# Four mask products ahead of four score products in the masked attention of a one-core Flamingo block

## The chip, the cores and the metric

The kernel runs on one core of a Trainium2 chip. The metric is the device time of one execution in microseconds. The engines of the core work side by side and meet through semaphores: TensorE (PE in the profile, its weight loads PEld), VectorE (DVE), ScalarE (ACT), GpSimd (POOL) and the queue of SyncE (SP), which here only starts transfers.

## What is computed

Four batches of 512 tokens with 256 features pass through four blocks in a row: a cross attention with 16 heads of 64, a grouped attention with a mixture of experts, a masked cross attention with 16 heads of 16 against 1601 context rows, and a self attention with experts. The change is in the third block:

```python
def _L1_xattn_ref(values, keys, queries, mask, w_out, b_out):
    ...
    energy = jnp.einsum('nqhd,nkhd->nhqk', q, k)
    energy = jnp.where(mask == 0, jnp.float32(-1e+20), energy)
    attn = jax.nn.softmax(energy / math.sqrt(EMBED), axis=3)
    out = jnp.einsum('nhql,nlhd->nqhd', attn, v).reshape(N, q_len, HEADS * HEAD_DIM)
    return out @ w_out.T + b_out
```

## The kernel before

The program is one list of units (`plan.order`), written once by `build_order`, and every engine walks through it in that order, each doing its own part of a unit. So the list is the order of the work on TensorE, and an engine that waits holds up everything behind it on that engine. `build_order` has generators, each a stream of units (scores of a block, products with the values, what prepares them), and `weave` takes from them by a string of digits: `TURNS_1` for the blocks 1 and 2, `TURNS_3` for the blocks 3 and 4, one digit for each unit. `Pace` keeps estimated times beside it (`Step(...)`: TensorE time, time on other engines, slots). They decide which of the three slots a unit takes (the one that comes free first) and how many `warm` products fill long gaps, not the order itself.

The scores and projections of all blocks share three slots of PSUM, the ring (`RING = 3`), each of two banks of 512 columns. A slot is free again when ScalarE or VectorE has read it.

Of block 3, for each of four batches and four groups of four heads:

- `max3` (32 units for a group): two heads' products of 128 queries with 401 keys in bf16, L1227, one slot; VectorE adds the mask and takes the maximum (L1679, two instructions for a unit), which frees the slot.
- `negb`, `strip`, `low`, `rowb` (L1219, L1246): make the row with the negated maxima, which goes into the queries as an extra feature.
- `scoreb` with blk 3, the masked tile (13 for a group, 208 in all): scores of up to 124 keys with 512 queries for four heads, in two slots, two heads in each. The heads' score products (L1266, 32 rows of the array for each head, fp32, two instructions for a product) run side by side in the four row strips. The mask is added by a product with a unit matrix on the whole array in bf16: L1259 for the heads 0 and 1, ahead of the scores, and L1272 for the heads 2 and 3, behind them. The wait for the second slot (`second_free`) stands between the score products of head 1 and head 2. ScalarE then takes the exponentials, one instruction for a slot (L1435).
- `pvb` with blk 3 (13 for a group): the product with the values, four heads in four strips of 32 columns (L1287). It takes no slot. It runs a tile or two behind the scores, since there are two buffers for exponentials.

Block 4 is woven into it, a batch behind: `maxb` (L1239), its own `scoreb` without a mask (4 for a group, the same L1266 with keys in `wide`), its `pvb`, and long stretches of whole-array products: `projqk` (L1195, L1196), `expert4` (L1366, L1367), `outb` (L1301).

TensorE works in three ways here: on the whole array, in four row strips (L1227, L1239, L1266) and in four column strips (L1287). Between two units of different ways it stands at a border, which the planner reckons with `DIVIDE`.

The tile in the code of before:

```python
                        for h in range(2):
                            pe.matmul(head_bank(unit, h), ident_b[0:kn, :], maskT_sb[0:kn, k, :],
                                      start=True, stop=False)
```

Of the kernel before, what the change touches and what calls it, by code (L numbers as in the profile page):

```python
# [21 lines left out]
GROUP = 4  # L22
PAD = P // GROUP
PAIRS = HEADS // 2
# [100 lines left out]
class Slots:  # L125
# [33 lines left out]

TURNS_3 = (
    "00333333333333333333333333333333333333333133301323132331332313231323313323133231332313233133233213031332332133"
    "13323133233133231332313323133233231333133233231102313323313323213310332331332313332313323133231332331332332130"
    "31332121032132332133133231323313323133231323313323133231332313023332133331023133233213323013412332114343323734"
    "27313341323413323132336142337132334231434334132334214734371323313323545324471363532441336413323134241435323313"
    "36532323336413343413423132313233321371363532353633133231332314231323313323133253634323431314243143532313323132"
    "33321336437146353241323313324142337471323536413231323332136341343343532353233361125363321363325713635323313633"
    "43612313233321124331343323733413424734132341332371423413324132341332361342334371335323313243713635332337136343"
    "34241335323414243713235323414365323363411323413234133256536341423413324133253641323413423333643331743243532341"
    "13233136353323413323361323371323332153234136337132341332532333413341423523361133653231323633713235323136313231"  # L170
    "32332513633436123142132334323173341334421424132413241323413324132314233725417142436132314235323413364133654241"
    "32413635323371323132333321433313231323332654171324146353235324471363313233713243713231324132337132413235363233"
    "43613314254125716546241421654214212446124121425216521125616225764644746447447447474744554645464546444674455464"
    "5464546444674454546445446464546575656576676"
)

# [140 lines left out]
def build_order(plan):  # L318
# [52 lines left out]
    def wide_prep():  # L371
        for b in range(B):
            for p in range(PAIRS):
                s, before = p % 2, pair_at(b, p, -2)
                gate = (("pva", *before, NKT - 1),) if before else ()
                if p == 0:
                    yield Step(use=(("ve", 4.2),), needs=gate, name=("ln", 1, b))
                    emit(on(("ln", 1, b), *free["xn_a"]))
                    yield Step(1.0, (("sc", 1.05),), 1, (("ln", 1, b),), ("turn", 1, b))
                    turn = emit(on(in_slot(("turn", 1, b), "scalar"), *free["xnT_a"]))  # L380
                    free["xn_a"] = (("tensor", turn),)
                for c in range(2):
                    yield Step(2.75, (("sc", 0.9), ("ve", 0.6)), 1, gate, ("kproj", b, p, c))
                    emit(on(in_slot(("kproj", b, p, c), "scalar"), *k_free[s], *free["kB"]))
                yield Step(1.75, (("sc", 0.6), ("ve", 0.45)), 1, (("turn", 1, b),), ("qproj", b, p))
                unit = emit(on(in_slot(("qproj", b, p), "scalar"), *k_free[s], *free["qB"]))
                if p == PAIRS - 1:
                    free["xnT_a"] = (("tensor", unit),)
                for q in range(QT):
                    for c in range(4):  # L390
                        yield Step(0.17, (("ve", 1.05),), 1, (("qproj", b, p),), ("maxa", b, p, q, c), (2, 2))
                        unit = emit(in_slot(("maxa", b, p, q, c), "vector"))
                free["kB"] = free["qB"] = (("tensor", unit),)
                yield Step(use=(("ve", 0.3),), needs=(unit,), name=("nega", b, p))
                emit(on(("nega", b, p), *free["col_a"]))
                yield Step(0.25, (("sc", 0.6),), 1, (("nega", b, p),), ("rowa", b, p))
                unit = emit(on(in_slot(("rowa", b, p), "scalar"), *neg_free[s]))
                free["col_a"] = (("tensor", unit),)
# [101 lines left out]
    def slim_scores(blk, b, g):  # L500
        tiles = NKT if blk == 3 else QT
        expo, before = {2: expo_2, 3: expo_3, 4: expo_4}[blk], group_at(b, g, -1)
        masks = (2.0, (1, 1), 1.5, 0.55) if blk == 3 else (0.88, (4, 4), 0.88, 0.0)
        for k in range(tiles):
            unit = ("scoreb", blk, b, g, k)
            behind = (b, g, k - 2) if k >= 2 else (*before, tiles + k - 2) if before else None
            yield Step(masks[0], (("sc", 1.02), ("sc", 1.02)), 2,
                       (("rowb", blk, b, g),) + ((("pvb", blk, *behind),) if behind else ()), unit, *masks[1:])
            in_slots(unit, "scalar_first", "scalar")
            i = expo.take()  # L510
            plan.slot[unit], plan.slot_free[unit] = i, expo.free[i]
            emit(unit)
        if blk != 2:
            (k3_free if blk == 3 else k4_free)[g % 2] = (("tensor", unit),)
# [241 lines left out]
def flamingo(nc, t, out):  # L756
    plan = Plan()
    order, bank_of, slot_of = plan.order, plan.bank, plan.slot
    ctx = ExitStack()
    with ctx:  # L760
# [216 lines left out]
        def head_bank(unit, h):  # L977
            return ring_t[:, bank_of[unit][h // 2], (h % 2) * BANK:(h % 2 + 1) * BANK]
# [94 lines left out]
        def _(pe):  # L1073
            past = Past(pe)
            past.wait_ge(*at("vector", "setup"))
            for unit in order:
# [171 lines left out]
                elif kind == "scoreb":  # L1248
# [6 lines left out]
                        past.wait_ge(*(at("scalar", "projk", b) if blk == 2 else at("scalar", "projqk", b, g)))  # L1255
                    if blk == 3:
                        past.wait_ge(*at("vector", "mask_keys"))
                        for h in range(2):
                            pe.matmul(head_bank(unit, h), ident_b[0:kn, :], maskT_sb[0:kn, k, :],  # L1259
                                      start=True, stop=False)  # L1260
                    for h in range(GROUP):
                        own = slice(PAD * h, PAD * h + PAD)
                        if h == 2:
                            for lane, other in plan.second_free[unit]:
                                past.wait_ge(*at(lane, *other))
                        last = pe.matmul(head_bank(unit, h), key_columns(blk, g, k0)[own, :],  # L1266
                                         queries_place(blk, g)[own, :], start=blk != 3 or h >= 2, stop=blk != 3 or h < 2)
                        if h == 1:
                            last.then_inc(tensor_done, 1)
                    if blk == 3:  # L1270
                        for h in range(2, GROUP):
                            last = pe.matmul(head_bank(unit, h), ident_b[0:kn, :], maskT_sb[0:kn, k, :],  # L1272
                                             start=False, stop=True)
                    last.then_inc(tensor_done, 1)
                elif kind == "pvb":
                    blk, b, g, k = a
# [679 lines left out]
```

## Time and profile before

| | us |
|---|---|
| median of 3 runs | 3478.32 (3477.23 to 3482.04) |
| the profiled execution | 3479.19 |
| its span | 3477.0 |
| first masked tile starts, last ends, from the span's start | 2127.6, some 3331 |
| PE busy | 3308.9 (95%) |
| DVE busy | 2020.1 (58%) |
| ACT busy | 1439.3 (41%) |

All rows come from the one profiled execution. A group's "busy" counts overlapping instructions of the group once, and a matmul's end is modelled, so the distance from start to start tells more of TensorE's pace than its busy share.

### The profile page before, as it was taken

To read this page: it belongs to the slowest core of one execution; us is meant where nothing else is said; L and a number is where in the kernel's file an instruction comes from.
4 is the path that set the end of the run, shared out by engine and by line. 5 is a ranking of instruction groups with operands and counts; after the bars stand their busy time and mean duration, and the time that the engine had idled before them with its cause. 6 is when DMAs were issued, how large, how long until landed. Compare 5 with 4: busy or idle time off the path is not lost.

```text
span 3477.0 us, 45530 instructions
## 1 busy us (share of the span) xinstructions
PE 3308.9 (95%) x18530; PEld 1442.0 (41%) x18530; DVE 2020.1 (58%) x4314; ACT 1439.3 (41%) x1645; POOL 957.2 (28%) x469
## 2 busy tenths in 40 slices
PE   7999999999999999999997979998999999999999
PEld 4444444444444445434442752223323343333354
DVE  4444445554665465565565027776767677666546
ACT  3443434444334443344433212454454435544434
POOL 4665555454465553554500000110000000000000
PEclk9999999999999999999999999999999999999999
DMA  4000000000000000000021430211111111110000
GB/s 154 11 13 13 32 8 11 13 7 32 8 19 11 13 26 8 25 10 8 4 97 49 125 108 18 60 39 49 35 35 36 35 29 25 51 35 26 13 19 13
DMA packets 68252, 114.94 MB, mean 33 GB/s; under 512 B 4849, under 2 KB 49545, under 8 KB 67530
## 3 DMA queue, kind: packets, MB, share of 16 engines
q1 hardware_dynamic: 62666, 97.08, 8.8%
q0 software_dynamic: 5376, 14.95, 1.9%
q8 instruction: 145, 2.38, 0.3%
q14 instruction: 65, 0.53, 0.0%
HBM read 101.79 MB, written 16.78 MB: 34 GB/s over the span
## 4 chain that ended last, share of the span: by engine, by line
PE 85%; DVE 7%; ACT 4%; POOL 2%; DMA 1%; issue 1%; ACTq 0%; DVEq 0%; POOLq 0%
PE ring L1266 10%; PE pv L1160 10%; PE ring L1149 9%; PE pv L1287 9%; PE ring L1227 3%; PE ring L1259 3%; PE ring L1121 3%; PE ring L1130 3%; PE ring L1122 3%; PE ring L1146 3%; PE ring L1107 3%; PE ring L1272 2%; PE ring L1108 2%; ACT wide L1435 2%; PE ring L1345 2%; PE ring L1326 2%
## 5 line engine op out<-in xcount | busy, mean ns | idle before, releaser
L1532 POOL TENSOR_TENSOR wide<-wide 124x1024 f32<-124x1024 f32 (+1 forms) x341 | 804.2, 2358 | 263.9 <-ACT wide L1428 227.7
L1435 ACT ACTIVATE wide<-ring 124x1024 f32<-124x1024 f32 (+2 forms) x544 | 528.5, 1022 | 549.4 <-PE ring L1266 547.0
L1651 DVE TENSOR_REDUCE max_a<-ring 128x2 f32<-128x802 f32 x512 | 491.9, 991 | 373.0 <-PE ring L1130 372.8
L1428 ACT ACTIVATE wide<-ring 124x1024 f32<-124x1024 f32 (+1 forms) x416 | 425.6, 1027 | 445.5 <-PE ring L1149 404.3
L1679 DVE CUSTOM_DVE_ANT_0 rest<-ring,slim 128x401 bf16<-128x401 f32 x683 | 374.3, 577 | 138.1 <-PE ring L1227 134.2
L1149 PE MATMUL ring<-wide 64*124 64x512 f32 (+1 forms) x1664 | 428.6, 593 | 0.0
L1160 PE MATMUL pv<-wide 124*64 124x512 f32 (+1 forms) x1664 | 413.0, 611 | 3.5 <-ACT wide L1428 3.5
L1689 DVE TENSOR_REDUCE slim<-ring 128x2 f32<-128x1024 f32 x256 | 307.5, 1221 | 111.6 <-PE ring L1239 110.3
L1266 PE MATMUL ring<-slim 32*128 32x512 f32 x2176 | 351.1, 646 | 3.0 <-DVE max_b L1679 2.3
L1502 POOL DMA_DIRECT2D slim<-in_ctx_k x16 | 8.8, 549 | 992.8 <-PE ring L1227 628.6
L1529 POOL TENSOR_TENSOR wide<-wide 124x1024 f32<-124x1024 f32 x31 | 73.4, 2369 | 557.9 <-ACT wide L1428 435.7
L1287 PE MATMUL pv<-wide,slim 124*32 124x512 f32 (+1 forms) x1664 | 223.8, 611 | 0.9 <-ACT wide L1435 0.9
L1679 DVE CUSTOM_DVE_ANT_0 slim<-ring,slim 128x401 bf16<-128x401 f32 x341 | 196.1, 575 | 46.9 <-PE ring L1227 45.4
L1160 PEld LDWEIGHTS pv<-wide 124*64 124x64 f32 (+1 forms) x1664 | 98.7, 136 | 225.4 <-issue 206.0
L1149 PEld LDWEIGHTS ring<-wide 64*124 64x124 f32 (+1 forms) x1664 | 156.7, 185 | 73.2 <-issue 50.2
L1227 PE MATMUL ring<-slim 32*128 32x401 bf16 x1024 | 157.8, 340 | 14.4 <-ACT wide L1435 10.7
L1130 PE MATMUL ring<-wide 64*128 64x401 bf16 x1024 | 154.8, 338 | 16.0 <-DVE max_a L1651 10.2
L1146 PE MATMUL ring<-wide,select_b 64*128 64x512 bf16 x832 | 160.1, 382 | 10.3 <-DVE max_a L1651 5.7
L1266 PEld LDWEIGHTS ring<-slim 32*128 32x128 f32 x2176 | 110.8, 184 | 139.5 <-issue 110.9
L1121 PE MATMUL ring<-wide 128*124 128x128 f32 (+1 forms) x832 | 165.9, 282 | 2.5 <-ACT wide L1424 1.8
L1122 PE MATMUL ring<-wide 128*124 128x128 f32 (+1 forms) x832 | 162.6, 277 | 0.0
L1435 ACT ACTIVATE slim<-ring 128x1024 f32<-128x1024 f32 x128 | 124.4, 1021 | 87.3 <-PE ring L1266 86.7
(239 smaller groups left out, 4096.2 us busy)
## 6 DMA issues: line engine op xcount, KB each, us to landing
slim<-in_ctx_k SPq DMA_DIRECT2D x16, 800.5 KB, 4.3
wide<-in_w_pair SPq DMA_DIRECT2D x32, 384.0 KB, 3.1
slim<-in_ctx_v SPq DMA_DIRECT2D x16, 744.0 KB
wide<-in_w SPq DMA_DIRECT2D x16, 512.0 KB, 4.8
wide<-in_we SPq DMA_DIRECT2D x16, 512.0 KB, 3.7
wide<-in_ctxT SPq DMA_DIRECT2D x4, 1601.0 KB, 6.6
slim<-in_ctx_k POOLq DMA_DIRECT2D x16, 400.2 KB, 4.7
wide<-padded_x SPq DMA_DIRECT2D x8, 640.0 KB, 4.8
```

What stands on the lines that cost most here:

```text
L1121: pe.matmul(place, ctxT[:, 0, k0:k0 + kn], pair_weights(p)[:, 2, 0, :], start=True, stop=False)
L1122: last = pe.matmul(place, ctxT[:, 1, k0:k0 + kn], pair_weights(p)[:, 2, 1, :], start=False, stop=True)
L1149: last = pe.matmul(slot[0:kn, h * BANK:(h + 1) * BANK], keys_a[own, p % 2, k0:k0 + kn], queries_a[own, p % 2, :], start=False, stop=True)
L1160: last = pe.matmul(pv_a[64 * h:64 * h + 64, :], values_a[0:kn, p % 2, k, 64 * h:64 * h + 64], exps_a[0:kn, slot_of["scorea", b, p, k], h * ...
L1266: last = pe.matmul(head_bank(unit, h), key_columns(blk, g, k0)[own, :], queries_place(blk, g)[own, :], start=blk != 3 or h >= 2, stop=blk ...
L1287: last = pe.matmul(pv_of[blk][PAD * h:PAD * h + PAD, :], value_columns(blk, g, k, kn, h), exps_tile(blk, b, g, k, h)[0:kn, :], start=k == ...
L1428: sc.activation(exps_a[0:kn, slot_of[unit], :], slot[0:kn, :], ACT.Exp, scale=WIDE ** -0.5).then_inc(scalar_done, 1)
L1435: sc.activation((exps_2 if blk == 2 else exps_34)[0:kn, first + 2 * i:first + 2 * i + 2, :].rearrange("p h n -> p (h n)"), ring_t[0:kn, ba ...
L1532: po.tensor_tensor(sums[0:kn, :], sums[0:kn, :], view, ALU.add).then_inc(pool_done, 1)
L1651: ve.reduce_max(max_a[:, :, q, c], slot.rearrange("p (h n) -> p h n", h=2)[:, :, 0:CHUNK], AX.X).then_inc(vector_done, 1)
L1679: ve.tensor_tensor_reduce(out=max_junk[junk], in0=slot[:, i * BANK:i * BANK + CHUNK], in1=maskQ_sb[:, q, CTX_CHUNKS[c]:CTX_CHUNKS[c] + CHUNK],
L1689: ve.tensor_reduce(neg_cols[blk][:, q, 2 * hp * PAD:2 * hp * PAD + PAD + 1:PAD], slot.rearrange("p (h n) -> p h n", h=2), AX.X, ALU.max, n ...
```

## The change

Of a masked tile all four mask products come first, then all four score products. The wait for the second slot moves with it, ahead of the mask product of head 2. The planner's entry for the tile is 1.86 instead of 2.0, its way of working at the end is four strips instead of the whole array, its first scores are counted from 1.86 instead of 1.5, and its second slot from 0.42 instead of 0.55. `TURNS_3` is another string. In `wide_prep` the first keys of a batch get one more condition (`held`) for the planner.

```diff
-        masks = (2.0, (1, 1), 1.5, 0.55) if blk == 3 else (0.88, (4, 4), 0.88, 0.0)
+        masks = (1.86, (1, 4), 1.86, 0.42) if blk == 3 else (0.88, (4, 4), 0.88, 0.0)
...
+                held = (("vproj", b - 1, PAIRS - 1, 1),) if b and p == 0 else ()
...
-                    yield Step(2.75, (("sc", 0.9), ("ve", 0.6)), 1, gate, ("kproj", b, p, c))
+                    yield Step(2.75, (("sc", 0.9), ("ve", 0.6)), 1, gate + held, ("kproj", b, p, c))
...
 TURNS_3 = (
-    "00333333333333333333333333333333333333333133301323132331332313231323313323133231332313233133233213031332332133"
...
+    "00333333333333333333333333333333333333333133313233132331332332313331323313323313323132331323032312330331332313"
...
                     if blk == 3:
                         past.wait_ge(*at("vector", "mask_keys"))
-                        for h in range(2):
+                        for h in range(GROUP):
+                            if h == 2:
+                                for lane, other in plan.second_free[unit]:
+                                    past.wait_ge(*at(lane, *other))
                             pe.matmul(head_bank(unit, h), ident_b[0:kn, :], maskT_sb[0:kn, k, :],
                                       start=True, stop=False)
                     for h in range(GROUP):
                         own = slice(PAD * h, PAD * h + PAD)
-                        if h == 2:
+                        if h == 2 and blk != 3:
                             for lane, other in plan.second_free[unit]:
                                 past.wait_ge(*at(lane, *other))
                         last = pe.matmul(head_bank(unit, h), key_columns(blk, g, k0)[own, :],
-                                         queries_place(blk, g)[own, :], start=blk != 3 or h >= 2, stop=blk != 3 or h < 2)
+                                         queries_place(blk, g)[own, :], start=blk != 3, stop=True)
                         if h == 1:
                             last.then_inc(tensor_done, 1)
-                    if blk == 3:
-                        for h in range(2, GROUP):
-                            last = pe.matmul(head_bank(unit, h), ident_b[0:kn, :], maskT_sb[0:kn, k, :],
-                                             start=False, stop=True)
                     last.then_inc(tensor_done, 1)
```

In the blocks 1 and 2 the order and the slots are as before. In the blocks 3 and 4 the number of each kind of unit is the same, except for two more `warm` units (together one product more).

Two places show the order on TensorE. The line numbers of the changed kernel: L1263 is the mask products, L1270 the score products, L1228 the maxima, L1287 the values still; an x2 of L1228 is one `max3` unit, an x4 two.

TensorE, batch 0, group 3, from the masked tile 3 on, before:

```order
L1259 MATMUL ring<-slim,ident_b 128x512 x2
L1266 MATMUL ring<-slim 128x512 x4
L1272 MATMUL ring<-slim,ident_b 128x512 x2
L1227 MATMUL ring<-slim 128x401 x2
L1287 MATMUL pv<-wide,slim 32x512 x4
L1227 MATMUL ring<-slim 128x401 x4
L1259 MATMUL ring<-slim,ident_b 128x512 x2
L1266 MATMUL ring<-slim 128x512 x4
L1272 MATMUL ring<-slim,ident_b 128x512 x2
L1227 MATMUL ring<-slim 128x401 x4
L1287 MATMUL pv<-wide,slim 32x512 x4
L1227 MATMUL ring<-slim 128x401 x2
```

The same tiles with the change:

```order
L1263 MATMUL ring<-slim,ident_b 128x512 x4
L1270 MATMUL ring<-slim 128x512 x4
L1228 MATMUL ring<-slim 128x401 x2
L1287 MATMUL pv<-wide,slim 32x512 x4
L1228 MATMUL ring<-slim 128x401 x4
L1263 MATMUL ring<-slim,ident_b 128x512 x4
L1270 MATMUL ring<-slim 128x512 x4
L1228 MATMUL ring<-slim 128x401 x2
L1287 MATMUL pv<-wide,slim 32x512 x4
L1228 MATMUL ring<-slim 128x401 x2
```

The scores now stand directly against the maxima, with no mask product between, and of the maxima one instead of two comes right behind a tile; two and three maxima for a tile take turns, where before most tiles of this place had three.

TensorE, batch 1, group 1, where a tile of block 4's scores (the L1270 with `wide`) follows a masked tile, with the change (before, this place had the same units between such a pair, at a tile two later in the group):

```order
L1263 MATMUL ring<-slim,ident_b 128x512 x4
L1270 MATMUL ring<-slim 128x512 x4
L1228 MATMUL ring<-slim 128x401 x2
L1287 MATMUL pv<-wide,slim 32x512 x4
L1228 MATMUL ring<-slim 128x401 x2
L1270 MATMUL ring<-wide 128x512 x4
```

Here the unit that follows takes two slots at once and starts both with its first products; it moved two tiles forward.

## Rows read from the trace of the kernel before

**Rows 1.** The page's busy line of TensorE: us, share, instructions.

```profile
PE 3308.9 (95%) x18530; PEld 1442.0 (41%) x18530; DVE 2020.1 (58%) x4314; ACT 1439.3 (41%) x1645; POOL 957.2 (28%) x469
```

**Rows 2.** Busy time of each engine in the masked half, granted clock, DMA share, GB/s.

```profile
2125.00:3332.00 1207.00, 1170.94 (x7045) 409.88 (x7043) 827.75 (x2532) 569.70 (x616) 31.75 (x38) 0.99 0.13 35
```

**Rows 3.** Groups by line in that stretch: busy us, mean ns, idle before, releasers.

```profile
L1435 ACT ACTIVATE wide<-ring 124x1024 f32<-124x1024 f32 (+2 forms) x510 | 495.5, 1022 | 535.6 <-PE ring L1266 533.4 <-PE ring L1272 1.7
...
L1266 PE MATMUL ring<-slim 32*128 32x512 f32 x1664 | 267.9, 643 | 2.3 <-DVE max_b L1679 2.3
...
L1227 PE MATMUL ring<-slim 32*128 32x401 bf16 x960 | 146.8, 340 | 13.9 <-ACT wide L1435 10.7 <-DVE slim L1710 1.2 <-DVE max_b L1679 0.5
L1272 PE MATMUL ring<-slim,ident_b 124*128 124x512 bf16 (+1 forms) x416 | 126.8, 387 | 0.0
L1259 PE MATMUL ring<-slim,ident_b 124*128 124x512 bf16 (+1 forms) x416 | 125.9, 384 | 4.5 <-ACT wide L1435 2.8 <-DVE max_b L1679 1.2
```

**Rows 4.** TensorE in order of time: start us, us, line, instructions, idle before and releaser.

```profile
2322.45 0.60 PE L1259 MATMUL ring<-slim,ident_b 124*128 124x512 bf16 x2
2322.99 1.14 PE L1266 MATMUL ring<-slim 32*128 32x512 f32 x8
2324.06 0.61 PE L1272 MATMUL ring<-slim,ident_b 124*128 124x512 bf16 x2
2324.60 0.34 PE L1227 MATMUL ring<-slim 32*128 32x401 bf16 x2
2324.87 1.07 PE L1287 MATMUL pv<-wide,slim 124*32 124x512 f32 x8
2325.87 0.69 PE L1227 MATMUL ring<-slim 32*128 32x401 bf16 x4
2326.49 0.60 PE L1259 MATMUL ring<-slim,ident_b 124*128 124x512 bf16 x2
2327.03 1.50 PE L1266 MATMUL ring<-slim 32*128 32x512 f32 x8
2328.45 0.60 PE L1272 MATMUL ring<-slim,ident_b 124*128 124x512 bf16 x2
...
2330.88 0.60 PE L1259 MATMUL ring<-slim,ident_b 124*128 124x512 bf16 x2
...
2333.73 0.34 PE L1227 MATMUL ring<-slim 32*128 32x401 bf16 x2 [0.29 <-ACT wide L1435]
```

**Rows 5.** ScalarE in the same stretch: both exponentials of the first two tiles.

```profile
2324.22 1.94 ACT L1435 ACTIVATE wide<-ring 124x1024 f32<-124x1024 f32 x2 [2.45 <-PE ring L1266]
2328.26 1.94 ACT L1435 ACTIVATE wide<-ring 124x1024 f32<-124x1024 f32 x2 [2.10 <-PE ring L1266]
```

**Rows 6.** VectorE there: first and last instruction of one unit of maxima.

```profile
2324.98 0.58 DVE L1679 CUSTOM_DVE_ANT_0 rest<-ring,slim 128x401 bf16<-128x401 f32 x1 [1.17 <-PE ring L1227]
...
2325.98 0.08 DVE L1679 DVE_READ_ACCUMULATOR2_ANT max_b<- 128x1 f32 x1
```

**Rows 7.** TensorE later: a mask pair with a whole-array product behind it.

```profile
2519.85 0.60 PE L1272 MATMUL ring<-slim,ident_b 124*128 124x512 bf16 x2
2520.29 1.02 PE L1219 MATMUL ring<-slim,consts 128*128 128x512 f32 x2
```

**Rows 8.** TensorE: unmasked scores of block 4 with maxima right behind them.

```profile
2509.61 1.14 PE L1266 MATMUL ring<-wide 32*128 32x512 f32 x8
2510.58 0.34 PE L1227 MATMUL ring<-slim 32*128 32x401 bf16 x2
```

**Rows 9.** TensorE: a masked tile and the block-4 tile that follows it.

```profile
2646.19 0.60 PE L1259 MATMUL ring<-slim,ident_b 124*128 124x512 bf16 x2
...
2649.84 1.22 PE L1266 MATMUL ring<-wide 32*128 32x512 f32 x8
```

**Rows 10.** TensorE's waits in the masked half: waiter, releaser, us, times, longest.

```profile
PE ring L1227 <- ACT wide L1435: 10.7, 32, 1.0
```

More of the change, by code:

```diff
@@ L161 @@
 TURNS_3 = (
-    "00333333333333333333333333333333333333333133301323132331332313231323313323133231332313233133233213031332332133"
[L163 to L171, printed above, removed]
@@ L172 @@
-    "32413635323371323132333321433313231323332654171324146353235324471363313233713243713231324132337132413235363233"
-    "43613314254125716546241421654214212446124121425216521125616225764644746447447447474744554645464546444674455464"
-    "5464546444674454546445446464546575656576676"
+    "00333333333333333333333333333333333333333133313233132331332332313331323313323313323132331032312330331332332313"
+    "33321331323313323313323323112013233133323023333110332331332313233133323321333133233133233133233133231332331230"
@@ new lines @@
+    "12312313233132331323313233321331332313233132313233103231323313321230331323313233132331332332133132330412334121"
+    "32331333432337461423413241423431424333413231323313234323413331323533313233143241323353365423734136341323433714"
+    "64334532333641323313235334132341363532341323353327136331323413353241323334142343744314243413231323132313633657"
+    "52323371364132313241463325713231323132413231323536413233637134333532331363532353233713631323132353631323363713"
+    "32336341421213234323373341334132373413241323313234132436142341324132343234134532313637132313233132437132335343"
@@ new lines @@
+    "43341323532437136413241324313635323132336571323332513633132331323373734132353464331231424314243413241323136353"
+    "23132431323365713231363323413353243713241324132313241324132413245132314633335324313233132313633265713635323532"
+    "31363136353231323633436412121323433374363347341324142341324132471423313343254132331363532414233132353231463413"
+    "23413233713233136433752433341324334132331323365217132313241324132413233132353631323136353235324136413241323334"
+    "14234412657121752121421426456121421421421462452146571625756257664644746447444744747445546454645464446744554645"
@@ L175 @@
+    "4645464446744745445446546454646575656576676"
 )
```

## The prediction

> **What bounds the kernel now.** The page's first section comes first: TensorE is busy for 95% of the span [rows 1], so the end is set there, and what counts is its pace and its waits. The change reorders only the half with blocks 3 and 4, so the next view is the table of stretches for the masked half: 1207 us, TensorE busy for 1170.94, VectorE 827.75, ScalarE 569.70 [rows 2]. That looks like an engine with nothing to give but its own work, but the groups by line say otherwise. The score products are busy for 267.9 us over 208 tiles, 1.29 us for a tile [rows 3], where an undisturbed tile shows 1.14 [rows 4]: 0.15 us for a tile, some 31 us, are a wait inside the tile, for the second slot, and the view of waits counts none of it, as busy time is modelled. The waits that it does count are small, the longest sum 10.7 us in 32 times [rows 10]. So two things share the limit: TensorE's own sequence, and the three slots of the ring.
>
> The timeline of TensorE shows both. From start to start a tile is 0.54 for the first mask pair, 1.07 for the scores, 0.54 for the second pair, 2.15 in all [rows 4]. Where whole-array work follows the second pair, the pair costs 0.44 [rows 7], and where maxima follow scores directly, the scores cost 0.97 [rows 8]. A border between two ways of working is thus some 0.10 us. One maxima unit is 0.27, one unit of the value products 1.00 [rows 4]. The next tile in that series waits: its scores take 1.50 busy instead of 1.14 [rows 4], for lack of the second slot.
>
> **What the change takes away on TensorE.** No product is added or removed. Two of the three borders around a tile may go. After the change a tile is 0.54 for the first masks, 0.44 for the other two (the price of a pair with its own kind behind), then 0.97 with maxima or unmasked scores behind, 1.07 with anything else: 1.95 or 2.05. Before, it is 2.15, or 2.05 with whole-array work behind. Which unit follows I counted in the two orders. Before: in 153 of 208 tiles strip work (maxima nearly always), in 18 value products, in 37 whole-array products: 171 x 2.15 + 37 x 2.05 = 443.5 us. After: 182 strip work, 18 value products, 8 whole-array: 182 x 1.95 + 26 x 2.05 = 408.2 us. The difference is 35.3 us. Whole-array units that stood behind a tile for free now stand elsewhere and bring borders of their own: the orders hold 1394 borders in this half before and 1064 after, 330 fewer, where the tiles alone lose 353. The 23 others give 2.3 us back. So 33.0 us of TensorE's sequence are gone, if nothing waits.
>
> **What it does to the ring.** A slot is held until it is read. Before, from the tile's start, the first exponential begins at 1.77 (2324.22 against 2322.45) and the two end at 3.71 [rows 4, 5]. A maxima unit that waited for the first slot began 2.85 after its tile (2333.73 against 2330.88) [rows 4], so slot one is free at 2.85, and slot two at 3.71 and the same 0.06 of passing on, 3.77. After the change the scores start 0.44 later, and both exponentials with them: 3.29 and 4.21. Slot two is also wanted sooner, at 0.44 instead of 0.54, since its masks come early. A tile holds its slots for 0.44 + 0.44 + 0.10 = 0.98 us longer, 204 us for 208 tiles, which over three slots is 68 us of the ring, twice what TensorE saves. What of it comes onto the path depends on what stands between two tiles, and I walked through the patterns. A maxima unit holds its slot from its start to the end of VectorE's last instruction, 1.46 (2326.06 against 2324.60) [rows 4, 6], 1.51 with passing on.
>
> Two maxima between tiles (scores, maxima, values, maxima; 43 times after, 19 before). Before: 2.15 + 0.27 + 1.00 + 0.27 = 3.69, and slot two is free at 3.77: a cycle of 3.77. After: 1.95 + 1.54 = 3.49, first slot at hand, second wanted at 3.93 and free at 4.21: 0.28 of waiting, again 3.77. The saving is gone whole.
>
> Two and three in turn, the first place shown in the change (three: 42 with the third behind the values, 5 otherwise). Before: after 3.77 the second cycle reaches 7.73, wants its second slot at 8.27 and has it at 8.70 when the second maxima unit is read: 8.16 for two. After: the second cycle would start at 7.60, waits for slot two until 7.98, then for the slot of the second maxima unit (free at 8.57, wanted at 8.42): 8.13. For three each time the trace has 4.39 (2330.88 against 2326.49) [rows 4], and the same walk gives 4.36 after. So 90 tiles of such short cycles lose 90 x 0.20 = 18.0 us of the saving and keep 90 x 0.015 = 1.3.
>
> A block-4 tile behind a masked one, with maxima, values, maxima between (17 after, 13 before). It takes two slots at once. Before it starts 3.65 after its masked tile and can have slot two at 3.77 [rows 9]; after, it stands ready at 3.49 and its heads 2 and 3 wait until 4.21. That loses the 0.20 and another 0.44: 17 x 0.64 = 10.9 us. This term is the least sure: its bounds are 17 x 0.20 = 3.4 us (other waits would have come anyway) and twice the 10.9, where the late block-4 tile makes the next masked one late too.
>
> The other tiles, some 100, stand in cycles with long whole-array stretches (experts, projections) or with the values alone; slots are free long before they are wanted there, and the saving stays.
>
> **Edits without a price.** The first half has the same order and the same slots, so the extra condition there costs nothing. ScalarE and VectorE do the same work; their busy sums in the masked half (569.70 and 827.75 of 1207 us) [rows 2] leave cover for any shift in their order. One warming product more is 0.2 us. Of the gathers and the low keys on GpSimd's queue one swap is made, with transfers that have many us to land at a DMA share of 0.13 [rows 2]. The buffers of keys and values are released by tiles whose order in their own stream is the same. The granted clock is 0.99 in this stretch [rows 2], the upper of the two levels (2.4 GHz), and nothing here lets TensorE rest longer.
>
> **The sum.** 33.0 - 18.0 + 1.3 - 10.9 = 5.4 us gained. Against the profiled execution, 3479.2, that is 3473.8, and since its time is 0.9 over the median of the runs, 3473 against 3478.3.
>
> **A rule that speaks against the change.** What the rows show is that the time from a score product to a free slot is ScalarE's, 1.94 us for two slots [rows 5], whatever TensorE does. The Trainium skill says it under TensorEngine Tiling, section PSUM Bottleneck, in my words: packing products into strips speeds the array, but not the reading of PSUM, which may become the limit. By that rule alone the masked half would not gain at all, which is the second rival; by the borders alone it would gain the whole 33 us, the first.
>
> **Rivals.** First: the ring does not take it back, because the new order was made with the tile's longer hold in mind and my walk takes every short cycle at its tightest. For it: two maxima between tiles stand where three stood, and one instead of two right behind the tile, so that fewer maxima wait for the first slot (the 10.7 us in 32 times [rows 10]). Against it: the walk of the very order shown ends at 8.13 and 8.16. It gives 25 to 33 us, about 3450.
>
> Second: reading sets the pace, the gain is wholly gone. The short cycles as above, and in the long ones the time freed before a stretch is waited off behind it. It gives no change, 3478.
>
> Third, slower: the wait for slot two, now ahead of all scores, delays both exponentials where before it delayed only the second. A late slot then makes the next slot late, and so on through a row of short cycles. The place is the masked tile's third mask product, above all behind block-4 tiles. Its price is the mean wait inside a tile: today 0.15 us. The saving of 33 us is 0.16 for a tile, so from a mean wait of 0.31 us on the change costs. My walk has 0.28 in the cycle with two maxima and 0.38 + 0.15 in the one with three, so it is near. At 0.40 for all tiles it is 208 x 0.25 - 33 = 19 us slower, 3497; at 0.35, 3487. Against it: half of the tiles are not in short cycles.
>
> That the change does not do what it says would be a border that stays between masks and scores of the same tile; that one is counted. The other borders vanish by construction.
>
> **How the numbers follow.** My forecast, most of the saving waited off, 3464 to 3481 around 3473: 0.45. First rival, 3445 to 3464: 0.17. Second, 3475 to 3482: 0.16. Third, 3485 to 3500: 0.22. A difference of 0.2%, 7 us, is about what a measurement of this kernel can tell from none. Of the forecast's case somewhat over half lies more than 7 us below, with the first rival 0.42 faster; slower is the third rival and a little of the forecast, 0.24; the rest is 0.34. For the range I take in the first rival down to 3447 and the third up to 3493, which leaves a tenth on either side.
>
> **What would show it.** In the profile after: a score group of 0.97 from start to start with maxima behind it, and mask groups of four with 0.98 to the scores; both exponentials 2.2 after the tile's start instead of 1.77; in the first place a pair of cycles of 8.1 us. Waits of TensorE for the exponentials move from the maxima into the mask products: over 30 us of idle time or stretched groups there. The masked half as a whole ends 5 us sooner. Wrong would be: tiles whose masks take no longer than 0.98 nearly everywhere (then the gain is near 33), or a mean stretch of the mask group by more than 0.3 (then it is slower).

## The result, and the profile after

The changed kernel takes 3524.44 us in the median (3518.02 to 3527.61) against 3477.78 for the kernel before: a ratio of 1.0134, 95% interval 1.0121 to 1.0146. It is 46.7 us slower, where 5 us faster was forecast and the range ended at 3493.

The masked half in the profile after, the table of stretches (us; busy time of each engine; clock; DMA), answers to [rows 2]; it lasts from 2128.1, the first masked tile, to some 3367:

```profile
2125.00:3369.00 1244.00, 1153.13 (x7002) 396.61 (x7001) 834.80 (x2530) 562.52 (x611) 32.03 (x39) 0.98 0.13 34
```

TensorE is busy for 1153 us instead of 1171, in a stretch that is 37 us longer. The granted clock is 0.98 against 0.99; what stands behind that small difference comes at the end of this section. The groups by line of that stretch (busy us, mean ns, idle before and releasers), to hold against [rows 3]:

```profile
L1270 PE MATMUL ring<-slim 32*128 32x512 f32 x1664 | 244.9, 659 | 0.0
L1263 PE MATMUL ring<-slim,ident_b 124*128 124x512 bf16 (+1 forms) x832 | 243.2, 391 | 40.0 <-ACT wide L1435 30.2 <-DVE max_b L1679 7.4
...
L1228 PE MATMUL ring<-slim 32*128 32x401 bf16 x960 | 149.4, 338 | 38.9 <-ACT wide L1435 34.1 <-DVE max_b L1679 3.0 <-ACT src L1400 0.6
```

Masks and scores together are busy for 488.1 us, where they were for 520.6. The idle time before masks rose from 4.5 to 40.0 us and before maxima from 13.9 to 38.9, and most of it (64.3 of the 78.9 us) ends with an exponential of ScalarE. Part of the rise before the masks is only the tile's old wait made visible: before, the wait for the second slot stood inside the scores, where idle time does not show it. The waits of TensorE by releaser (total us, times, longest), against [rows 10]:

```profile
PE ring L1228 <- ACT wide L1435: 34.1, 39, 1.7
PE ring L1263 <- ACT wide L1435: 30.2, 52, 4.2
```

The view of waits still leaves out what hides inside a group. So I took every unit's start in the trace and set against each distance the shortest one that the same kind of neighbours shows; what is over counts as a wait. The split between the two depends by a few us on which distances are compared. From the first masked tile's start to the last one's, the kernel before has 1200.1 us, of which 147.3 are waits; the changed one has 1235.6, of which 219.6 are waits. TensorE's own sequence went from 1052.8 to 1016.0 us, 36.8 less, and the waits rose by 72.3. Behind the last masked tile's start the span has 149.4 us before and 159.8 after, another 10.4.

The series that the forecast walked through, batch 0, group 3, shows TensorE (start us, us, line, instructions, idle):

```profile
2350.06 1.25 PE L1263 MATMUL ring<-slim,ident_b 124*128 124x512 bf16 x4
2351.24 1.14 PE L1270 MATMUL ring<-slim 32*128 32x512 f32 x8
2352.21 0.33 PE L1228 MATMUL ring<-slim 32*128 32x401 bf16 x2
2352.48 1.06 PE L1287 MATMUL pv<-wide,slim 124*32 124x512 f32 x8
2353.55 0.52 PE L1228 MATMUL ring<-slim 32*128 32x401 bf16 x4
2354.46 1.21 PE L1263 MATMUL ring<-slim,ident_b 124*128 124x512 bf16 x4 [0.40 <-ACT wide L1435]
...
2358.20 1.03 PE L1263 MATMUL ring<-slim,ident_b 124*128 124x512 bf16 x3
```

and ScalarE beside it:

```profile
2352.47 1.94 ACT L1435 ACTIVATE wide<-ring 124x1024 f32<-124x1024 f32 x2 [1.83 <-PE ring L1270]
2356.84 1.94 ACT L1435 ACTIVATE wide<-ring 124x1024 f32<-124x1024 f32 x2 [2.44 <-PE ring L1270]
```

The scores cost 0.97 with maxima behind them. The two cycles take 4.40 and 3.74, 8.14 together (8.13 was forecast). The masks of both tiles are stretched by a late second slot (1.18 and 1.15 to the scores instead of 0.97), and the first exponential comes 2.41 and 2.38 after the tile's start, against 1.77 in [rows 5]; a tile that gets its slot in time shows 2.20. So here the walk was right. The loss is elsewhere, for instance where two maxima follow a tile:

```profile
2148.68 1.14 PE L1270 MATMUL ring<-slim 32*128 32x512 f32 x8
2149.64 0.33 PE L1228 MATMUL ring<-slim 32*128 32x401 bf16 x2
2150.99 0.50 PE L1228 MATMUL ring<-slim 32*128 32x401 bf16 x4 [1.01 <-ACT wide L1435]
2151.91 1.21 PE L1263 MATMUL ring<-slim,ident_b 124*128 124x512 bf16 x4 [0.41 <-ACT wide L1435]
```

The second maxima unit can only have the tile's first slot, and stands for 1.01 us; in [rows 4] the same place stood for 0.29 (2333.73). Then the next tile stands for another 0.41.

Not everything that I counted as a wait is one. The records of the granted clock have 27.3 us at 0.50 in the masked half before and 54.6 us after. One such stretch of the changed kernel, with TensorE in it:

```profile
2227.40:2237.60 10.20, 8.54 (x34) 1.88 (x38) 6.55 (x27) 1.94 (x2) 0.00 (x0) 0.50 0.00 1
```

```profile
2228.21 0.52 PE L1228 MATMUL ring<-slim 32*128 32x401 bf16 x2 [2.34 <-DVE max_b L1679]
2228.66 1.89 PE L1263 MATMUL ring<-slim,ident_b 124*128 124x512 bf16 x4
2230.48 2.09 PE L1270 MATMUL ring<-slim 32*128 32x512 f32 x8
```

Just before, TensorE had stood for 1.68 and 2.34 us. The tile then takes 3.69 us from start to start (to 2232.35) instead of 1.95, on the lower of the two levels (1.2 instead of 2.4 GHz). Of the waits above, some 26 us of the 219.6 lie in stretches at 0.50, and 10 of the 147.3 before, so up to 16 of the 72 us more are products at the lower level that came with the new waits.

### The profile page after: what moved, and what is told of

It is laid out like the page before. It is cut to its first block, busy times and chain, and to the rows that moved or that the text cites. A ratio compares the mean times of both kernels' runs of the same rounds, so it can differ in the third digit from the quotient of the medians.

```text
span 3523.5 us, 45530 instructions
## 1 busy us (share of the span) xinstructions
PE 3300.5 (94%) x18531; PEld 1432.9 (41%) x18531; DVE 2027.9 (58%) x4314; ACT 1435.1 (41%) x1643; POOL 956.7 (27%) x469
## 3 DMA queue, kind: packets, MB, share of 16 engines
q8 instruction: 145, 2.38, 0.3%
## 4 chain that ended last, share of the span: by engine, by line
PE 82%; DVE 8%; ACT 6%; issue 1%; POOL 1%; DMA 1%; SPq 0%; DVEq 0%; ACTq 0%; POOLq 0%
PE ring L1270 11%; PE pv L1161 10%; PE ring L1150 9%; PE pv L1287 7%; PE ring L1263 6%; ACT wide L1435 4%; PE ring L1122 3%; PE ring L1131 3%; PE ring L1123 3%; PE ring L1147 3%; PE ring L1108 3%; PE ring L1109 2%; PE ring L1228 2%; PE ring L1345 2%; PE ring L1326 2%; PE ring L1366 2%
## 5 line engine op out<-in xcount | busy, mean ns | idle before, releaser
L1270 PE MATMUL ring<-slim 32*128 32x512 f32 x2176 | 328.0, 658 | 0.7 <-DVE slim L1704 0.4
L1263 PE MATMUL ring<-slim,ident_b 124*128 124x512 bf16 (+1 forms) x832 | 243.2, 391 | 40.0 <-ACT wide L1435 30.2
L1287 PE MATMUL pv<-wide,slim 124*32 124x512 f32 (+1 forms) x1664 | 224.9, 613 | 0.0
L1228 PE MATMUL ring<-slim 32*128 32x401 bf16 x1024 | 160.7, 338 | 39.4 <-ACT wide L1435 34.1
L1228 PEld LDWEIGHTS ring<-slim 32*128 32x128 bf16 x1024 | 47.5, 92 | 279.6 <-ACT wide L1435 173.7
```

Source lines behind the costliest of these rows:

```text
L1228: last = pe.matmul(slot[:, i * BANK:i * BANK + CHUNK], queries_low(3, g)[own, q * P:(q + 1) * P], keys_low(3, g)[own, CTX_CHUNKS[c]:CTX_CH ...
L1287: last = pe.matmul(pv_of[blk][PAD * h:PAD * h + PAD, :], value_columns(blk, g, k, kn, h), exps_tile(blk, b, g, k, h)[0:kn, :], start=k == ...
```

## Experiments: the form and the order apart

Three theories stood against each other. A, the ring: exponentials that start 0.44 us later bring waits that cost more than the borders give. B, the order: the tile's new form is good, the new order is bad. C, the moved wait: since the masks of heads 2 and 3 now stand ahead of all scores, a late second slot holds up the first exponential too, which the planner does not know (`Pace.accept` adds the wait to the tile's end, but counts the first exponential from the tile's start).

**The form alone.** The tile as in the changed kernel, string of turns and planner numbers as before, so that order and slots are those of before (the diff is against the changed kernel, cut):

```diff
-    "00333333333333333333333333333333333333333133313233132331332332313331323313323313323132331323032312330331332313"
+    "00333333333333333333333333333333333333333133301323132331332313231323313323133231332313233133233213031332332133"
...
-        masks = (1.86, (1, 4), 1.86, 0.42) if blk == 3 else (0.88, (4, 4), 0.88, 0.0)
+        masks = (2.0, (1, 1), 1.5, 0.55) if blk == 3 else (0.88, (4, 4), 0.88, 0.0)
```

> All four mask products ahead of the scores, but with the order and the slots of the kernel before (its string of turns and its planner numbers). Theory A (the ring: exponentials start 0.44 us later, so slots come free later, and the waits that this brings are more than the 33 to 37 us that TensorE saves): no faster than before, between 3480 and 3525 us, with the sum of borders gone and more waiting of maxima for the first exponential. Theory B (the new order is to blame, the form is good): faster than before by most of the borders, 3445 to 3460.

Measured: 3583.14 us, ratio 1.0293 (1.0271 to 1.0315), 105 us slower than before. Theory B in its plain form is refuted, and A's own figure was too small by more than half. Its waits from 2120 to 3345 us (its masked half ends at some 3436):

```profile
PE ring L1228 <- ACT wide L1435: 73.7, 87, 1.7
PE ring L1263 <- ACT wide L1435: 18.7, 42, 1.1
```

**The order alone.** The new string of turns with the tile of before (the diff is the mirror image of the last, without the tile's code).

> The new order with the tile as before (two masks, four scores, two masks). Theory A: the order is made for a tile whose slots come late and suits the old tile no worse than its own old order, 3475 to 3495. Theory B: the order itself has the loss, so the old tile in it is as slow as or slower than the changed kernel, 3520 to 3560, since the borders come back on top.

Measured: 3507.10 us, ratio 1.0076 (1.0058 to 1.0093), 29 us slower. That lies between the theories. Of these 29, the part behind the last masked tile's start is 161.1 against 149.4 us, so 12, and the masked half is 17.5 longer (1217.6 against 1200.1), of which 12 to 17 are waits, by the distances compared. The new order is thus a poor one for the old tile, but the form costs 105 in the old order and only 17 in the new.

| | old order | new order |
|---|---|---|
| two masks, scores, two masks | 3478 | 3507 |
| four masks, scores | 3583 | 3524 |

**Late exponentials alone.** The kernel before, with nothing changed on TensorE; the first exponential waits for the tile's end:

```diff
-                        past.wait_ge(*at(("tensor_first", "tensor")[i], *unit))
+                        past.wait_ge(*at(("tensor" if blk == 3 else "tensor_first", "tensor")[i], *unit))
```

> The kernel before in everything that TensorE does, but the first exponential of a masked tile waits until the whole tile is done, not for its heads 0 and 1, so both exponentials come 0.4 to 0.5 us later, as in the changed kernel. Theory A: this delay alone costs 25 to 60 us, 3503 to 3538. Theory B: ScalarE is idle half of the time, the delay is covered, under 7 us.

Measured: 3582.55 us, ratio 1.0296 (1.0279 to 1.0313), 104 us slower, where theory A's span ended at 60. Both exponentials begin 0.54 us later here (2.24 to 2.31 after the tile's start in an undisturbed tile, against 1.70 to 1.77), and a tile then costs 0.50 us more on average. ScalarE is idle for more than half of the masked half, and that covers next to nothing of it. The waits by releaser (2120 to 3345 us again) show the same place as with the form alone:

```profile
PE ring L1227 <- ACT wide L1435: 66.5, 87, 1.5
PE ring L1259 <- ACT wide L1435: 10.0, 30, 0.6
```

This run is the proof for the main point: nothing but the start of the exponentials was changed, and the kernel loses 104 us. The form alone, with the same order and the same slots, ends within 1 us of it, although it has fewer borders. The busy time of TensorE, 1194.52 us with late exponentials and 1165.75 with the masks first in the same stretch of 1310 us, does not measure that, since it holds the waits inside the scores. By starts, TensorE's own sequence is 33 us shorter with the masks first and its waits are 31 us longer. But the two are no clean pair for the borders: the delay is 0.43 us with the form alone and 0.54 here, the form alone also has the moved wait (next run), and it wants the second slot 0.10 sooner. Nor do the parts add up. An estimate in proportion to the delay gives 104 x 0.43 / 0.54 = 83 us, with 20 for the moved wait and 33 off for the borders 70, where the form alone costs 105. What makes the other 35 stays open.

**The wait alone.** The kernel before, with the second slot's wait ahead of head 0's score product:

```diff
-                        if h == 2:
+                        if h == (0 if blk == 3 else 2):
```

> The kernel before with one wait moved: the wait for the second slot of a masked tile stands ahead of the score product of head 0, no longer between heads 1 and 2. TensorE issues the same products in the same order, and a tile that gets its slot in time is unchanged; in the 100 tiles that wait there (32 us in all) the first exponential is now late by the wait as well. Theory C (the planner lets the first exponential run on during the wait, while with the masks first it cannot): 15 to 40 us slower, 3493 to 3518. Theory A in its plain form (only the fixed 0.44 us counts): within 7 us of before.

Measured: 3501.07 us, ratio 1.0056 (1.0040 to 1.0073), 20 to 23 us slower, within theory C's span. The products, their order and the price of an undisturbed tile are those of before. So theory C holds as a part of the loss, measured with the old tile in the old order: to let 100 late tiles hold up their first exponential too costs about two thirds of what those waits themselves are. The groups by line show the wait, which was invisible inside the scores (267.9 busy, 2.3 idle [rows 3]), as idle time, and maxima that wait longer:

```profile
L1266 PE MATMUL ring<-slim 32*128 32x512 f32 x1664 | 238.6, 643 | 24.2 <-DVE max_b L1679 19.0 <-ACT wide L1435 2.9 <-DVE slim L1689 0.8
...
L1227 PE MATMUL ring<-slim 32*128 32x401 bf16 x960 | 151.2, 341 | 26.5 <-ACT wide L1435 23.4 <-DVE slim L1710 1.5 <-DVE max_b L1679 0.5
```

## Experiments: the delay taken away

**Short exponentials.** Kernel before and changed kernel, both with exponentials of block 3 that take 384 of 1024 columns of a slot, so that most of the result is left out:

```diff
-                                      ring_t[0:kn, bank_of[unit][i], :], ACT.Exp,
+                                      ring_t[0:kn, bank_of[unit][i], 0:wide_c], ACT.Exp,
```

> The kernel before, but the exponentials of block 3 take only 384 of the 1024 columns of a slot, so part of the result is left out and ScalarE frees each slot some 0.6 us sooner. Only the base for the next one; with TensorE's sequence as the limit in most places, 3450 to 3475.

> The changed kernel with the same short exponentials (part of the result left out). Theory A and C: with slots that come free in time the saving of the borders shows, so it is 20 to 37 us faster than the kernel before with short exponentials, where with full ones it is 46 us slower. Theory B (the new order is bad in itself): still slower than that one, by 10 us or more.

Measured: 3461.36 us for the kernel before so shortened, ratio to the true one 0.9949 (0.9933 to 0.9966), and 3475.54 for the changed kernel, 0.9990 (0.9981 to 1.0000). The changed kernel is then 14 us slower instead of 47: two thirds of its loss hang on the time that ScalarE holds a slot. The expected gain of 20 to 37 did not come; 14 us slower is what theory B had said (10 or more), so ScalarE's hold of the slots is not the whole cause. Between the starts of the first and the last masked tile it is 1182.4 us against 1184.6, a gain of 2, and the rest behind it is 163.4 against 149.6, a loss of 14. In that rest stand 7.5 us of work that the new order puts there (below), and 28.7 us at a granted clock of 0.50 against 13.4.

The view of waits names the masks that wait for maxima, which VectorE has to read:

```profile
PE ring L1263 <- DVE max_b L1680: 26.8, 60, 1.5
```

In the kernel before with short exponentials the like of it (its L1259) is 3.9 us. But that is again the hidden wait made visible: there the scores are busy for 280.2 us in place of some 237 (208 tiles of 1.14). By starts, the waits inside the masked tile are nearly alike, some 47 us before and 52 after. What grew is the waiting of maxima behind maxima, from some 16 to 46 us. So even with a fast ScalarE this form in this order does not gain. How much of the 14 us is the order and how much the form no run separates, as the new order was not run with the old tile and short exponentials.

**Masks last.** The same borders can go in the other way: four scores first, four masks behind them, the first exponential after the masks of heads 0 and 1.

```diff
...
+                                         queries_place(blk, g)[own, :], start=True, stop=blk != 3)
...
+                    if blk == 3:
+                        for h in range(GROUP):
+                            last = pe.matmul(head_bank(unit, h), ident_b[0:kn, :], maskT_sb[0:kn, k, :],
+                                             start=False, stop=True)
+                            if h == 1:
+                                last.then_inc(tensor_done, 1)
```

> The order and slots of before; the four score products come first and all four mask products behind them, heads 0 and 1 signalled after their masks. The same borders are saved as in the changed kernel (about 33 us), the first exponential should begin about 1.8 us after the tile's start, as before (1.77), the second slot is wanted 0.54 us sooner. Theory A: most of the saving stays, 3445 to 3470. Theory B says nothing against it either, but by it e1 is as fast.

Measured: 3556.01 us, ratio 1.0222 (1.0205 to 1.0239), 78 us slower; the expectation missed. A tile with its slots in time does show its first exponential at 1.72, but the median is 2.19: the second slot is wanted at once, and 162 of 208 tiles wait for it inside the scores, 105 us in all against 35 in the kernel before. The groups by line show it as busy time of the scores (its L1263), 336.3 us against 267.9 [rows 3]:

```profile
L1263 PE MATMUL ring<-slim 32*128 32x512 f32 x1664 | 336.3, 642 | 8.1 <-ACT wide L1434 3.5 <-DVE max_b L1678 3.1
```

**Other orders.** I mended the planner so that a late second slot delays the first exponential, searched an order in which each tile may have either form, and another with all masks first.

```diff
-                end += max(0.0, self.ring[self.picked[1]] - at - step.second)
+                stall = max(0.0, self.ring[self.picked[1]] - at - step.second)
+                end += stall
+                if step.parts == (1, 4):
+                    at += stall
```

> The planner is mended so that a late second slot delays the first exponential of a tile with its masks first, and under it a new order is searched in which each of the 208 tiles may have either form; 56 take the masks first. What is asked is whether the form can be used with profit somewhere. If a saved border is worth its 0.1 us where slots are not wanted at once, 3465 to 3480, within 10 us of the kernel before; if the form costs wherever it stands, 3490 or more.

> All 208 tiles with the masks first, as in the changed kernel, and its order searched on under the mended planner. Theory C (the planner's blind spot led the order astray): it gets back part of the 46 us, 3495 to 3518, and no order of this kind reaches the kernel before, since the slots are held longer in any of them. If the order was at fault alone, below 3478.

Measured: 3499.37 us for the mixed one, ratio 1.0059 (1.0043 to 1.0076), and 3538.24 for masks first throughout, 1.0168 (1.0151 to 1.0185). The second is slower than the changed kernel itself, so the blind spot of theory C is real, but it is not shown that it led the order astray: a planner that knows of it picked a worse order. Nor does the mixed one show that the form costs wherever it stands, as was expected from 3490 up: its order is new as well, and was not run with the old tile. In its profiled execution (3491.85 us) the masked half is 7 us longer than before, and the rest behind it 8. No order that I tried makes the form pay, and none beats the kernel before. Whether one exists is open.

## Why the prediction was wrong, point by point

**TensorE's borders.** 33.0 us were forecast. The sequence in the masked half is 36.8 shorter by the trace, some 7 of it moved behind the last masked tile (below). With the old order and the form alone, where nothing moved, it is 33 shorter. This term held.

**The delay.** 0.44 us for both exponentials: 2.20 against 1.77 in an undisturbed tile. Held, in size; what it costs was not.

**The short cycles.** 8.13 forecast, 8.14 measured in the place shown. Over all cycles of two maxima, from the last score product of one tile to that of the next, 3.72 us before and 3.75 after; of three with one in front, 4.43 and 4.54. From start to start the two average 3.69 and 4.55 after the change, 8.24 for a pair, 0.1 over the forecast, so that the one place agrees to 0.01 us is in part luck. Held within some 0.1.

**The block-4 tile behind a masked one.** Its heads 2 and 3 were to come 0.44 us later, counted from the start of the masked tile. Over the places with maxima, values, maxima between, the last score product of the block-4 tile comes 4.33 us after that start before (13 places) and 4.88 after (17), 0.55 more. The place was right, the size a little small. All waits inside block-4 tiles rose from 5.3 to 17.8 us.

**The step that failed** is "The other tiles, some 100, stand in cycles with long whole-array stretches (experts, projections) or with the values alone; slots are free long before they are wanted there, and the saving stays." It was never read from rows. Some 20 of them are not even such tiles, but have two maxima right behind the tile. And the slots are not free in time. The cleanest measure is the form alone against the kernel before, as both have the same units between the same tiles. How much longer a cycle from tile to tile has become depends on the instruction it is counted from, so here are two:

| what stands between | cycles | longer, start to start | longer, last score product to last |
|---|---|---|---|
| whole-array work | 67 | 0.56 us each, 37.7 in all | 0.59 each, 39.5 in all |
| two maxima at once, short | 48 | 0.79, 38.0 | 0.84, 40.2 |
| maxima, values, maxima | 19 | 0.08, 1.6 | 0.18, 3.5 |
| other short ones with maxima | 39 | 0.43, 16.7 | 0.12, 4.7 |
| a block-4 tile | 22 | 0.39, 8.5 | 0.45, 9.9 |
| values alone, or nothing | 12 | 0.10, 1.1 | 0.49, 5.9 |

Where a saving of 0.20 each was forecast, the cycles with whole-array work lose 0.56 each (0.63 with late exponentials alone). The pattern that the walk had come out even, maxima, values, maxima, does so nearly. I had priced the patterns that stand most often in the new order, and let the rest have no price, although the prediction had itself worked out that a tile holds its slots 0.98 us longer, 68 us of the ring in all and twice what TensorE saves. That the new waits are 72 us is chance: the form alone holds the slots for just as much longer, and its waits rise by some 137. In the trace of the changed kernel they are: maxima behind maxima 39.3 to 58.9, inside the masked tile 34.6 to 51.2, masks behind maxima 4.6 to 21.3, block-4 tiles 5.3 to 17.8, and small ones.

**The clock.** The words "nothing here lets TensorE rest longer" failed with it: the new waits are such rests, and the time at 0.50 in the masked half doubled, 27.3 to 54.6 us (88.7 with the form alone; 64.8 with late exponentials alone, where TensorE's products are those of before).

**The work behind the last masked tile.** "Edits without a price" left out what the new order puts there: TensorE's lines from the end of the last masked tile hold 80 instead of 72 products of L1366 and 152 instead of 136 score products of block 4. That is one expert's unit and two tiles of block 4 with their values, 7.5 us by their rows, and the stretch is 10.4 longer; it also has 19.5 us at a granted clock of 0.50 against 13.7. I compared the counts of units for the whole half, where they are equal, and not for its end.

**The rivals.** The third had the mechanism: the wait ahead of all scores delays both exponentials. Its point from which the change costs, a mean wait of 0.31 us inside a tile, was meant for that wait alone. The trace has 51.2 us in the masks of 208 tiles, 0.25. That is below that point, and below the 0.3 that the prediction had named as the sign of a slower kernel. Yet it costs, since of the 72 us of new waits only 17 are inside the tile; the others are outside it, for its slots, by maxima and by block 4. By rights it should have been priced by everything that waits for the tile's slots. The first rival, that the order takes up the longer hold, is half true: it takes up 59 of the 105 us that the form costs in the old order. The second, no change at all, had the reading of slots as what sets the pace, but that reading also came later, which makes it a loss. Part of the 46.7 us is not the form's: the order alone costs 29 with the old tile, 12 of them behind the last masked tile.

**The rule on reading PSUM** (the Trainium skill, TensorEngine Tiling (Array Packing), section PSUM Bottleneck) points the right way. A reader of PSUM that is short of time in all, which the rule has in view, the trace does not show: ScalarE is busy for 562.52 of 1244 us. The late exponentials show that it matters when a slot's reading can begin (104 us), and the short ones that it matters how long it takes (the loss goes from 47 to 14).

## What to carry to other kernels

Where units share few buffers, price an edit by how long it holds them, and by everyone who queues for them, before counting what it saves on the busiest engine: here 0.54 us more from a tile's start to its first exponential cost 104 us with no work added, half a microsecond for a tile on average. A wait that stands in the middle of a unit may be worth its place: what stands ahead of it runs on, and so does the engine behind that. Moved ahead, it cost 20 to 23 us here. And when a hand walk agrees with the row to 0.01 us but covers half of the places, the other half needs a price too, or the range has to have its full width.

## What was not expected of the hardware

Busy time of matmuls hides waits inside a group of instructions, so idle time before a group can rise just because a wait moved out of another: the score products' 267.9 us became 238.6 when their wait was moved ahead of them, with 24.2 idle, and 336.3 where the second slot was wanted sooner, for the same 1664 instructions of 0.64 us. A border between the whole array and four row strips costs about 0.10 us from start to start (0.97 against 1.07 behind the scores, 0.44 against 0.54 behind a mask pair), in both kernels.
